# A two-layer graph attention on one NeuronCore: in the first attention, one mask product for both heads of a tile, and the denominator products of two tiles behind each other

## The reference, cut to what matters

```python
x_l = (x @ W + b).reshape(N, NHEADS, C)            # N 4096, NHEADS 8, C 64
alpha_l = jnp.einsum('nhc,hc->nh', x_l, att_l)
alpha_r = jnp.einsum('nhc,hc->nh', x_l, att_r)
scores = alpha_l[:, None, :] * alpha_r[None, :, :]
scores = jnp.where(adj[:, :, None] > 0, scores, NEG_INF)
att = jax.nn.softmax(scores, axis=1)
out = jnp.einsum('ijh,jhc->ihc', att, x_l)
return jax.nn.relu(out.reshape(N, NHEADS * C))
```

## Time and profile before

| | |
|---|---|
| Median of three runs | 4316.33 us (4311.41 to 4319.59) |
| Span of the profiled execution | 4310.4 us |
| First attention in it (16 groups, 64 blocks) | 1399.0 us, from 394.5 to 1793.5 |
| Period of a group | 87.42 us |
| Granted TensorE clock over the first attention | full (1.00, the 2.4 GHz level) |

### The profile page before, as it was taken

How to read it: one execution, slowest core, us unless ns; L and a number is a source line. 1 busy time by engine, 2 the same in 40 slices (tenths; PEclk the granted TensorE clock), 3 DMA queues, 4 the chain that set the end, 5 groups by cost and what they waited for, 6 DMA issues and landing times. The chain is left out here.

```text
span 4310.4 us, 61471 instructions
## 1 busy us (share of the span) xinstructions
PE 4049.2 (94%) x20713; PEld 1380.5 (32%) x20713; DVE 3693.9 (86%) x3590; ACT 2579.5 (60%) x2427; POOL 284.5 (7%) x300
## 2 busy tenths in 40 slices
PE   7887999999999999876999999999999999999977
PEld 5563222222222222253332323323233232323335
DVE  5556999999999999787998989989899898989966
ACT  3445888888888888513555555555555555555520
POOL 3331000000000000152000000000000000000000
PEclk9998999999999999866999999999999999999975
DMA  7884111111111111273111111111111111111133
GB/s 273 281 287 137 40 47 44 39 39 45 46 40 39 39 49 44 84 242 109 47 44 35 47 47 47 42 37 47 45 49 42 38 45 47 47 49 40 39 108 137
DMA packets 267044, 323.69 MB, mean 75 GB/s; under 512 B 21952, under 2 KB 193984, under 8 KB 266944
## 3 DMA queue, kind: packets, MB, share of 16 engines
q1 hardware_dynamic: 235968, 254.37, 19.5%
q0 software_dynamic: 13824, 42.35, 2.7%
q10 hardware_dynamic: 17152, 25.43, 1.7%
HBM read 262.70 MB, written 59.38 MB: 75 GB/s over the span
## 5 line engine op out<-in xcount | busy, mean ns | idle before, releaser
L1038 ACT ACTIVATE a_weights<-a_psS,a_shift 128x1024 f32<-128x1024 f32 x1024 | 1084.7, 1110 | 931.3 <-PE a_psS L972 930.4
L1078 DVE TENSOR_TENSOR a_weights<-a_weights,maskT 128x1024 f32<-128x1024 f32 x1024 | 1206.1, 1219 | 224.6 <-ACT a_weights L1038 220.4
L477 ACT ACTIVATE g_weights<-al_bc,g_shift,g_xl 128x1024 f32<-128x1024 f32 x1024 | 1187.8, 1231 | 166.9 <-DVE g_total L523 81.2
L516 DVE TENSOR_TENSOR g_weights<-g_weights,maskT 128x1024 f32<-128x1024 f32 x1024 | 1175.5, 1217 | 97.4 <-ACT g_weights L477 96.2
L972 PE MATMUL a_psS<-a_q,a_k 128*128 128x512 f16 x4096 | 977.6, 381 | 37.6 <-DMA a_k<-k_scratch 17.7
L568 PE MATMUL a_psO<-a_weights,a_v 128*64 128x512 f32 x4096 | 991.8, 605 | 9.0 <-DVE a_weights L1078 9.0
L568 PE MATMUL g_psO<-g_weights,g_xl 128*64 128x512 f32 x4096 | 965.9, 603 | 17.9 <-DVE g_weights L516 17.8
L972 PEld LDWEIGHTS a_psS<-a_q,a_k 128*128 128x128 f16 x4096 | 359.1, 98 | 820.6 <-issue 451.2
L568 PEld LDWEIGHTS g_psO<-g_weights,g_xl 128*64 128x64 f32 x4096 | 258.7, 136 | 703.0 <-issue 400.1
L1093 DVE TENSOR_TENSOR a_total<-a_total,a_weights 128x1024 f32<-128x1024 f32 x384 | 461.9, 1216 | 0.0
L568 PEld LDWEIGHTS a_psO<-a_weights,a_v 128*64 128x64 f32 x4096 | 248.3, 136 | 568.6 <-issue 496.3
(11 more groups left out here) (136 smaller groups left out, 1850.3 us busy)
## 6 DMA issues: line engine op xcount, KB each, us to landing
adj_sb<-in_adj_dram SPq DMA_DIRECT2D x128, 512.0 KB, 5.9
g_xl<-xl_scratch SPq DMA_DIRECT2D x128, 260.0 KB, 2.9
a_k<-k_scratch SPq DMA_DIRECT2D x256, 128.0 KB, 2.9
a_v<-in_L_gnn_v_dram SPq DMA_DIRECT2D x128, 256.0 KB, 2.8
al_bc<-alpha_scratch SPq DMA_DIRECT2D x16, 1024.0 KB, 5.0
f_oT<-o_scratch SPq DMA_DIRECT2D x16, 1024.0 KB
a_q<-q_scratch SPq DMA_DIRECT2D x64, 256.0 KB, 4.7
xl_scratch<-xl_sb POOLq DMA_DIRECT2D x32, 260.0 KB, 3.9
```

Source lines behind the costliest of these rows:

```text
L477: nc.scalar.activation(w[:, u % NP, h, :], al_bc[:, par, h, :], ACT.Exp, bias=shift_bc[:, par, h:h + 1], scale=xl[:, slot, u % KB, 2 * C + ...
L516: nc.vector.tensor_tensor(w[:, u % NP, h, :], w[:, u % NP, h, :], maskT[:, ds(q * JB + u, 1), ds(ic * IC, IC)] .rearrange("p a c -> p (a c)"),
L1038: nc.scalar.activation(w[:, u % NP, h, :], psS[h][:].rearrange("p a c -> p (a c)"), ACT.Exp, bias=shift_bc[:, par, h:h + 1], scale=SCALE). ...
L1078: nc.vector.tensor_tensor(w[:, u % NP, h, :], w[:, u % NP, h, :], maskT[:, ds(q * JB + u, 1), ds(ic * IC, IC)] .rearrange("p a c -> p (a c)"),
```

## The change

VectorE now masks both heads of a tile with one TENSOR_TENSOR of 2 x 1024, whose mask operand is the same 1024 bytes read for either head (`to_broadcast`); it waits for both ACTIVATEs of the tile, and `masked` counts tiles instead of heads. TensorE's order in a block becomes V0 V1 W0 W1 V2 V3 V4 V5 W4 W5 T V6 V7 W6 W7. `w_used` of places 2 and 3 still counts behind V; for the others it counts behind their W, which now comes after the next tile's V.

```diff
-                            for h in range(2):
-                                dve.wait_ge(exped, (B * JB + u) * 2 + h + 1)
-                                nc.vector.tensor_tensor(w[:, u % NP, h, :], w[:, u % NP, h, :],
-                                                        maskT[:, ds(q * JB + u, 1), ds(ic * IC, IC)]
-                                                        .rearrange("p a c -> p (a c)"),
-                                                        ALU.mult).then_inc(masked, 1)
+                            dve.wait_ge(exped, (B * JB + u) * 2 + 2)
+                            nc.vector.tensor_tensor(w[:, u % NP, :, :], w[:, u % NP, :, :],
+                                                    maskT[:, ds(q * JB + u, 1), ds(ic * IC, IC)]
+                                                    .to_broadcast([P, 2, IC]), ALU.mult).then_inc(masked, 1)
                             if u == SECOND + 1:
                                 dve.wait_ge(total_used, B)
-                                dve.wait_ge(masked, (B * JB + SECOND) * 2 + 2)
+                                dve.wait_ge(masked, B * JB + SECOND + 1)
...
-                            pe.wait_ge(masked, n * 2 + 2)
+                            pe.wait_ge(masked, n + 1)
                             last = add_values(nc, w[:, u % NP, :, :], xl[:, slot, u % KB, 0:2 * C], psO[par])
-                            if u not in (FIRST, SECOND):
-                                last = add_weights(nc, w[:, u % NP, :, :], psD[par], onesF)
-                            last.then_inc(w_used[u], 1)
-                            if u == SECOND + 1:
+                            if u in (FIRST, SECOND):
+                                last.then_inc(w_used[u], 1)
+                            elif u % 2 == 1:
+                                for t in (u - 1, u):
+                                    add_weights(nc, w[:, t % NP, :, :], psD[par], onesF).then_inc(w_used[t], 1)
+                            if u == SECOND + 2:
                                 pe.wait_ge(added, B + 1)
                                 add_weights(nc, total, psD[par], onesF).then_inc(total_used, 1)
```

## The result

The changed kernel takes 4514.47 us (median of four runs, 4509.55 to 4518.73) against 4314.81 for the kernel before on the same chips: 199.7 us slower, a ratio of 1.046 (95% interval 1.0446 to 1.0475). The forecast was 4505 in a range of 4450 to 4600.

A forecast was written before the change was run, and what follows sets the result against it. TensorE was taken as the bound before; after the change a ring of waits costs 162 us and clock falls 27, together 189, so 4316 + 189 = 4505 us, range 4450 to 4600.

The forecast's parts named there:

- The bound before: First attention before the change: TensorE is the bound, busy 86.75 of a group's 87.43 us; all others run in its slack.
- TensorE's price list: TensorE's start-to-start costs in the first attention: V 1.715 us, W 0.86, a pair of switches between them 0.29.
- The mask product: VectorE's two-head product: 2.20 us between starts instead of 2 x 1.135; the gain of 0.5 us a block worth nothing.
- rival 3: Reading the mask twice doubles VectorE's product to 4.4 us, time near 5340 us; chance 0.03.
- The lap: Per block, W0's end through tile 4's exponentials, masks, sum and V5 to the next W0: 24.06 us against TensorE's 20.6.
- The uncertain link: ScalarE's start of tile 4 after W0's end: 0.07 us taken; the other end, 0.26, would add 12 us.
- A group's start: First block of a group: `clear` adds 0.75 us and the evacuation 0.59, so a group takes 97.6 us against 87.4.
- the ring: Closed chain of waits across TensorE, ScalarE and VectorE, one lap a block; with group starts it costs 162 us more.
- The clock: TensorE's gap between V4 and V5 drops its clock in one block of four: 16 x 1.7 = 27 us.
- Rival 1: TensorE's clock falls in every block of the first attention, adding 109 us instead: 4587 us; chance 0.10.
- Rival 2: TensorE stays the bound and the saved switches decide: 56 us faster, 4260 us; chance 0.05.
- Rival 4: Switches and new waits cancel, or the instructions come out as before: 4316 us; chance 0.03.

The follow-up runs named there:

- late_pair_heads: Kernel before, one mask product for each head, with only tiles 6 and 7 paired (V6 V7 W6 W7): 4296.53 against 4314.42 us.
- mask_only: Kernel before with the two-head mask product and TensorE's old order: 4329.23 against 4314.07 us.
- order_only: Kernel before with TensorE's new order and one mask product for each head: 4457.19 against 4314.07 us.
- w4_first: Changed kernel with W4 put ahead of V5: 4423.24 us against 4314.07 for the kernel before.
- filler_full: Changed kernel with tile 4's denominator products done once more behind V4 into a spare bank: 4478.86 us against 4313.58 for the kernel before.
- sum45: Kernel before with tiles 4 and 5 summed instead of 2 and 3, sum behind mask 6, tiles 0 and 1 paired: 4284.86 against 4314.42 us.
- w0_first: Changed kernel without the pair of tiles 0 and 1 (V0 W0 V1 W1): 4487.44 us against 4312.69 for the kernel before.

## Why the prediction was right, step by step

**The bound before** and **TensorE's price list** stood. One saved pair of switches brought 17.9 us in `late_pair_heads` (64 x 0.29 = 18.6 by the list). The rule of the Trainium skill that a change of tiling mode drains the array (TensorEngine Tiling (Array Packing), Key Properties) agrees with these 0.28 us a pair; it was not what decided.

**The mask product** was taken at 2.20 between starts and 2.28 in length; behind the sum mask 5 starts 2.20 us later (881.03 to 883.24), and a product takes 2.29. The repeated operand costs nothing, so rival 3 falls.

**The lap** was forecast at 24.06 and measured at 24.07. (The TensorE links as listed add up to 14.69, not 14.67; that is 1 us in the whole kernel.) The idle time was forecast at 3.45 a block, with 2.5 between V4 and V5. The records show waits of 0.56 and 2.47, but a record is longer than the step to the next one. From start to start V4 comes 4.21 us after V2 instead of 3.43, and V5 4.41 after V4 instead of 1.715: 3.47 us together. The uncertain link, tile 4's start after W0, came at 0.07, the value taken. The halves test the formula with other numbers: 20.94 below TensorE's work in `mask_only`, 23.07 in `order_only`, 23.21 in `w4_first`.

**A group's start** was forecast so that a group takes 97.6; in `filler_full`, without falls, it takes 97.63. The 162 us for the ring are 164 in the trace after (203.0 less 39 for the falls) and 165 in `filler_full`.

**The clock** is the term that was mis-sized. I took one block in four, 16 falls at 1.7 us, 27 us. There are 24, at 1.64 each (blocks of 25.71 beside 24.07), 39 us. The row it was taken from, one fall after seven gaps of that length in the second attention, gave no frequency: one in seven would have been 9 falls and 15 us, every block 109. The reason given for one in four, that V4 waits just ahead of the gap, is not borne out: in `order_only` V4 does not wait, and there are 25 falls. So the number was a guess, and that it came within 12 us is luck; the 162 us of the ring, which decide the result, are not. What sets how often the clock falls stays open.

In the traces the ring and the falls are 2 and 12 us more than forecast, 203 against 189. The medians differ by only 199.7 us; the spans of the two profiled executions differ by 203.7, and these 4 us lie within the scatter of 8 to 9 us that the executions of either kernel show.

**One sign did not come as written.** TensorE's busy time in the stage was to go down by the switches saved; from the first to the last matmul of the stage it went from 1391.8 to 1405.9 us. The records are longer at half clock: in `w4_first`, which saves two of the three pairs of switches and has no falls, it is 1375.7. The share fell to 87%, for which some 85% had been said.

**Rival 1**, a fall in each block, did not come about. By the prediction the Trainium skill would have made it the forecast (TensorE: Matmul & The Clock Gate, HAM oscillation — how this bites in real kernels). But that section tells of waits of about 3 to 5 us that put the clock down in each turn; here a wait of 2.47 us did so in 24 turns of 64. So the section says less about this kernel than the prediction made of it.

**Rival 2** (TensorE stays the bound, 56 us faster) needed a lap under 20.6. Where the ring is shorter than TensorE's work, in `late_pair_heads` and `sum45`, its mechanism works as described. **Rival 4** (no change) is ruled out by the interval, 1.0446 to 1.0475.

A small slip: I put 5.9 us between the span and the time. The profiled run after took 4515.95 us at a span of 4514.1, so 1.9 us lie around it; the rest was the scatter of the runs. It did not enter the difference of 189.

## What to carry to other kernels

Before work is moved to save an engine's switches, follow each buffer once around: from the instruction that frees it, through everyone who refills it, back to that instruction. If that lap, with the move in it, is longer than the busiest engine's work per turn, the difference is lost in every turn, however idle the other engines look, and a link that is taken out may be a wait of the next ring. Here the same saving paid at the pair whose delay the ring did not feel (17.9 us), and more once the summed tiles were chosen so that no sum stood between masks 4 and 5 (29.6 us).

## What the runs showed of the hardware that was not expected

TensorE's clock fell to its 1.2 GHz level in a loop whose longest idle stretch was 2.47 us of 24, in 24 of 64 turns, each time for 3.41 us, at a price of 1.64 us. In `w0_first`, with 2.05 us of 23.16, it fell in 20 of 48 such turns. Four bf16 matmuls of one row of zeros in that stretch, busy 1.03 us in the records, left 18 falls; eight records of full-height fp32 products, 1.06 us, left none. Whether the number of rows, the data type or the zeros make the difference was not tried. The busy row of the profile does not tell them apart.
